# Mixture-of-experts stage of an audio tower: the search for tokens in two halves of eight experts, gathers of one half beside the search of the other

## The reference

```python
def _L0_ffn_ref(x, gate_w, w1, b1, w2, b2, sw1, sb1, sw2, sb2):
    ...
    logits = jnp.einsum('gsd,de->gse', xg, gate_w)
    probs = jax.nn.softmax(logits, axis=-1)
    flat_probs = probs.transpose(2, 0, 1).reshape(En, T)
    scores, tok_idx = jax.lax.top_k(flat_probs, cap)
    xf = x.reshape(T, Dn)
    toks = xf[tok_idx]
    h = jax.nn.gelu(jnp.einsum('ecd,edh->ech', toks, w1) + b1[:, None, :])
    y = jnp.einsum('ech,ehd->ecd', h, w2) + b2[:, None, :]
    y = y * scores[..., None]
    routed = jnp.zeros_like(xf).at[tok_idx.reshape(-1)].add(y.reshape(-1, Dn))
    shared = jax.nn.gelu(xf @ sw1 + sb1) @ sw2 + sb2
    out = (routed + shared).reshape(Bn, Sn, Dn)
```

## Time and profile before

| | |
|---|---|
| time, median of 3 runs | 1312.71 us (1312.13 to 1312.76) |
| the profiled execution | 1312.21 us |
| its span, first to last instruction | 1310.5 us |
| PE busy | 1181.3 us, 90% |
| DVE busy | 893.2 us, 68% |
| ACT busy | 733.1 us, 56% |
| POOL busy | 405.4 us, 31% |
| mean granted PE clock | 0.958 of full speed |
| block three begins | at 1002.7 us of the span |

### The profile page before, as it was taken

The page is one execution under the profiler, slowest core; times in us unless marked ns, Lnnn a source line. Parts: engine busy times, 40 slices in busy tenths (PEclk is TensorE's granted clock), DMA queues, the critical chain, the costliest instruction groups (busy, mean ns, idle before and its releaser), DMA issues. The chain is left out here.

```text
span 1310.5 us, 23146 instructions
## 1 busy us (share of the span) xinstructions
PE 1181.3 (90%) x7812; PEld 992.7 (76%) x7812; DVE 893.2 (68%) x2614; ACT 733.1 (56%) x1847; POOL 405.4 (31%) x379
## 2 busy tenths in 40 slices
PE   6999999999988999999999999999996998766663
PEld 6999999999966777777777777777764767555553
DVE  5656566656659898898998888988864887222120
ACT  2444534444448888888888888888882342222220
POOL 5000001202003442333344324231111001788885
PEclk9999999999999999999999999999997999878876
DMA  5100000000000000000000000000002110445442
GB/s 141 33 13 23 15 16 21 13 24 13 1 25 13 11 16 27 26 26 27 26 20 15 21 27 26 25 14 12 11 21 56 30 33 20 83 91 91 90 90 22
DMA packets 91799, 42.92 MB, mean 33 GB/s; under 512 B 31066, under 2 KB 88007, under 8 KB 91687
## 3 DMA queue, kind: packets, MB, share of 16 engines
q1 hardware_dynamic: 67207, 33.49, 9.4%
q0 software_dynamic: 23808, 6.69, 4.0%
q10 hardware_dynamic: 672, 1.31, 0.3%
HBM read 28.22 MB, written 9.65 MB: 29 GB/s over the span
## 5 line engine op out<-in xcount | busy, mean ns | idle before, releaser
L492 PE MATMUL bank<-h1hl,W2hl 128*128 128x376 f32 x1536 | 277.1, 336 | 2.9 <-DVE h1hl L648 2.9
L492 PEld LDWEIGHTS bank<-h1hl,W2hl 128*128 128x128 f32 x1536 | 263.4, 189 | 7.4 <-issue 4.3
L228 POOL TENSOR_SCALAR cellmax<-grid,csb 125x375 f32<-125x375 f32 x96 | 121.1, 1272 | 392.9 <-DVE csb L221 336.8
L1095 ACT ACTIVATE P<-P,nmax 125x375 f32<-125x375 f32 (+2 forms) x384 | 189.0, 509 | 2.4 <-DVE nmax L1236 2.2
L592 ACT ACTIVATE h<-bank,b2c 128x375 f32<-128x375 f32 x128 | 73.5, 575 | 207.1 <-PE bank L492 207.1
L1236 DVE CUSTOM_DVE_ANT_0 P<-bank,nbias 125x375 f32<-125x375 f32 (+2 forms) x384 | 139.0, 411 | 12.0 <-PE bank L913 12.0
L1105 ACT COPY PT<-bank 128x500 f32<-128x500 f32 (+1 forms) x256 | 128.5, 556 | 8.6 <-PE bank L926 7.9
L913 PE MATMUL bank<-QK 64*125 64x375 f32 (+2 forms) x768 | 116.2, 406 | 13.0 <-DVE nmax L1236 13.0
L926 PE MATMUL bank<-ident,P 125*128 125x125 f32 x768 | 113.5, 275 | 0.2 <-ACT PT L1105 0.2
L1714 ACT ACTIVATE hE<-bank,EB 128x375 f32<-128x375 f32 x64 | 36.7, 573 | 135.0 <-PE bank L1663 132.3
L1121 ACT ACTIVATE tap<-bank,qkd 128x375 f32<-128x375 f32 x128 | 68.5, 570 | 65.3 <-PE bank L962 65.2
(11 more groups left out here) (218 smaller groups left out, 2264.1 us busy)
## 6 DMA issues: line engine op xcount, KB each, us to landing
X<-in_x_dram SPq DMA_DIRECT2D x31, 375.0 KB
EW<-in_L_ffn_w_dram SPq DMA_DIRECT2D x32, 256.0 KB
token_table<-row SPq DMA_DIRECT2D x16, 210.9 KB
tTall<-tT SPq DMA_DIRECT2D x16, 187.5 KB, 2.5
out_dram<-oS SPq DMA_DIRECT2D x15, 187.5 KB
tTall<-in_L_tok_W_dram ACTq DMA_DIRECT2D x1, 1024.0 KB, 8.9
EB<-in_L_ffn_b_dram SPq DMA_DIRECT2D x16, 62.5 KB
tok<-token_table,ids POOLq DMA_INDIRECT x48
```

Source lines behind the costliest of these rows:

```text
L228: nc.gpsimd.tensor_scalar(cellmax[:, k % 2], grid0[:], csb[:, TT_ + k:TT_ + k + 1], None, ALU.max).then_inc(s_cm, 1)
L492: last = nc.tensor.matmul(bank[4 + m % 2][:, :NE], W2hl[:, a, k, m * 128:(m + 1) * 128], h1hl[:, p, b, k], start=(k == 0 and n == 0), stop ...
L1095: nc.scalar.activation(P[:, 2 * r + q, SEG[i]:SEG[i] + w], P[:, 2 * r + q, SEG[i]:SEG[i] + w], ACT.Exp, bias=nmax[:, 2 * r + q, i:i + 1], ...
```

## The change

- Two halves: `GE` = 8 experts each. `probsT` has a partition for each of 8 experts and 16 sequences, 2 x 375 columns, one half of the experts beside the other. Each sequence's probabilities are stored by two DMAs. Search, selection and lists are made for half 0, then for half 1, each over 375 columns (`over`, `tied`, `ties`, `chosen`, `place`); `hotA` and `hotB` are made for 384 columns once per half.
- `STEP_UNITS` puts 1 or 2 shared units between totals in the first search (after `FIRST_UNITS` = 2 ahead of the first total), 2 in the second; 7 stand beside the one-hot matrices of half 0.
- GpSimd issues the 24 gathers of half 0 at once when its lists are ready (`RING` = 8 buffers). The gathers of half 1 go two per expert behind the scatters of experts 2 to 13.
- Lists of half 1: the selection comes ahead of expert 0; `hotA`, `hotB` and `pass_tiles` stand between DVE's steps of experts 0 and 1, and `collect`, `transpose_lists`, `make_indices` on TensorE between experts 1 and 2.
- Experts: no run-time loop. The first layer uses two PSUM banks in turn, the second layer two others: third 0 in one, thirds 1 and 2 in the other. The bias is a matmul with a row of ones on TensorE. DVE multiplies by the score, read in place from `tok`, on the way from PSUM, third by third, and a scatter waits for its own third. No copies of indices or scores.
- Shared sums go from PSUM into `Hall` by DVE and are stored from there; `oS` and ScalarE's copies are gone.
- In block two `shared_y` stands after the projection (h = 3 of the last round) and no longer after the logits (h = 7).

```diff
+                        if (b, h) == (B, 3):
+                            shared_y(0, 0)
+                            shared_y(0, 1)
...
-                        if (b, h) == (B, 7):
-                            shared_y(0, 0)
-                            shared_y(0, 1)
...
-                        sp.dma_start(probsT[m // 2 * E:(m // 2 + 1) * E, m % 2 * N:(m % 2 + 1) * N], pTs[:]
-                                     ).then_inc(s_ps, 16)
+                        for half in range(2):
+                            sp.dma_start(probsT[m * GE:(m + 1) * GE, half], pTs[half * GE:(half + 1) * GE]
+                                         ).then_inc(s_ps, 16)
...
-            STEP_UNITS = [(k + 1) * 45 // STEPS for k in range(STEPS)]
+            FIRST_UNITS = 2
+            STEP_UNITS = ([FIRST_UNITS + 3 * (k + 1) // 2 for k in range(STEPS)],
+                          [33 + 2 * (k + 1) for k in range(STEPS)])
+            LIST_UNITS = ((25, 32, 33), (UNITS,))
+            B_FROM = 2
...
-                for e in range(AHEAD):
-                    gather(e, e)
+                for n in range(NT * GE):
+                    gather(n // NT, n % NT)
...
+                for e in range(E):
+                    scatter(e)
+                    for n in range(2 * (e - B_FROM), 2 * (e - B_FROM + 1)):
+                        if 0 <= n < NT * GE:
+                            gather(GE + n // NT, n % NT)
...
+                def second_layer(e):
+                    u = e % 2
+                    pe.wait_ge(s_ehr, 4 * e + 4)
+                    for t in range(NT):
+                        y = Y_B[min(t, 1)][:PT_, t * C:(t + 1) * C]
+
+                        if t < 2:
+                            wait(pe, s_ys, NT * (e - 1) + 1 if t == 0 else NT * e)
+                        for k in range(DC):
+                            nc.tensor.matmul(y, hE[:, u, k, t * PT_:(t + 1) * PT_], EW2[:, u, k], start=(k == 0),
+                                             stop=False)
+                        last = nc.tensor.matmul(y, ones_r[0:1, 0:PT_], EB2[0:1, u], start=False, stop=True)
+                        if t != 1:
+                            last.then_inc(s_ey, 1)
+
+                def expert(e):
+                    first_layer(e)
+                    if e + 1 < E:
+                        transpose_tokens(e + 1)
+                    second_layer(e)
...
+                transpose_chosen(1)
+                transpose_tokens(0)
+
+                pe.wait_ge(s_yr, NB)
+                expert(0)
+                expert(1)
+                collect(1)
+                transpose_lists(1)
+                make_indices(1)
+                for e in range(2, E):
+                    expert(e)
...
+                select(1, added, NB)
+                split_places(1)
+                take_tokens(0)
+                hot_a(1)
+                take_tokens(1)
+                hot_b(0, SLOT // 2)
+                weigh(0)
+                hot_b(SLOT // 2, SLOT)
+                take_tokens(2)
+                pass_tiles(1)
+                weigh(1)
+                pick(1)
+                for e in range(2, E):
+                    if e + 1 < E:
+                        take_tokens(e + 1)
+                    weigh(e)
```

588 lines of the change are left out of this document (265 added, 323 removed).

## The result

| | before | after |
|---|---|---|
| time, median | 1312.74 us (4 runs: 1312.13 to 1317.06) | 1331.63 us (4 runs: 1325.8 to 1334.56) |
| ratio | | 1.0131, interval 1.0088 to 1.0175 |
| the profiled execution | 1312.21 us | 1325.8 us |
| its span | 1310.5 us | 1324.1 us |
| mean granted TensorE clock | 0.958 | 0.959 |

The change costs 18.9 us by the medians and 17 by the ratio, which is one of means. It went the way that was forecast, but 15 us further, and above the upper end of the range (1326). The profiled execution is the fastest of the four after; the others are slower, and their mean clock is lower (1329.5 at 0.956, 1333.7 at 0.951, 1334.6 at 0.950). So the miss has two parts: 9.4 us inside the profiled execution (1325.8 against 1312.2 is +13.6, forecast +4.2), and 5.8 us from it to the median, where 0.5 was allowed.

A forecast was written before the change was run, and what follows sets the result against it. TensorE was taken to bound the search and GpSimd's scatter and gather rounds the expert stage. 1312.2 - 3.2 (block start) + 7.1 (to first scatter) - 0.2 (rounds) + 0.5 (port) = 1316.4, median 1316.9 us; range 1307.5 to 1326.

The forecast's parts named there:

- Block start: Third block's start, with shared_y moved behind the last projection: 3.2 us earlier.
- rival 3: Second search: DVE's cand and thr held by gathers, 13 us more, 1329; chance 0.07.
- Rounds with two gathers: Expert stage: the scatter's landing shows behind two gathers, 10.55 us a round, 1.0 less than before.
- rival 1: Expert rounds: gathers hide the scatter's dispatch, round 9.98 us, 1309.6 in all, if idle is under 0.4; chance 0.14.
- First late round: Round to scatter group 13, waiting for expert 14's last gather behind group 12: 15.3 us.
- Start to first scatter: From block start through two searches and lists to the first scatter: 7.1 us later than before.
- End just in time for the third group: Rest of hotB, second lists and collect, between experts 0 and 2, finish without delaying the third scatter group.
- The last rounds: Last three scatter rounds, two of them late for tokens of experts 14 and 15: 15.3, 17.6 and 11.3 us.
- the two other thirds of the layer: Second layer in the late groups: these come later than GpSimd would take them, 0.7 us per group.
- the port: DVE's small operations beside gathers in the second search: 0.5 us more.
- twelve rounds win 12.2 and two lose 11: First to sixteenth scatter group: 170.8 us for 170.98, so 0.2 us less.
- Rival 4: First search: TensorE at the low clock for half the steps, 10 us more, 1327; chance 0.05.

The follow-up runs named there:

- r9_warm: Changed kernel with eight matmuls whose result nobody reads in TensorE's waits beside the lists and before expert 0's first layer; 1326.88 us, ratio 1.0084 to the kernel before.
- r8_lists3: Changed kernel with the second half's collect, transposes and indices one expert later, between experts 2 and 3; 1329.05 us, ratio 1.0099 to the kernel before.
- r6_nobias: Changed kernel without its bias matmuls, the second bias left out of the result; 1325.33 us, ratio 1.0075 to the kernel before.
- r1_same: The changed kernel again, unaltered; 1334.12 us, ratio 1.0128 to the kernel before.
- r2_tail: Changed kernel with three gathers behind experts 2 and 3, then two, the last behind expert 12 instead of 13; 1322.21 us, ratio 1.0045 to the kernel before.
- r10_best: Changed kernel with the edits of r2_tail, r8_lists3 and r9_warm, and one more unread matmul behind each collect; 1312.78 us, ratio 0.9987 to the kernel before.
- r12_fills: r9_warm's kernel with one more unread matmul behind each half's collect; 1329.70 us, ratio 1.0104 to the kernel before.
- r3_fill: Changed kernel with unread matmuls in the first search, behind the two first totals and in steps with one shared unit; 1334.47 us, ratio 1.0138 to the kernel before.

## Why the prediction was wrong

The step that failed is the price of TensorE's work behind a wait. The sum put the first lists and expert 0's first layer at the high clock, took what stands ahead of expert 2 to be hidden, and gave the last two thirds of a late expert's layer 0.7 us. The rows show the first at the low clock (3.5 us more up to the first scatter), the second on the path (2.5 us more in the second round), and 3.0 us for the third, with its bias matmuls.

**Right:** the sign, and the structure of the sum. Block start: 3.2 us earlier was forecast; shared_y alone gave 2.4 of the time. The 4.3 of the profile has 1.7 of spread in it, since the projection ended that much earlier than in the profile of before. The second search took 40.0 us for 14 steps with 24 gathers beside it, to the tenth as computed. The counts took 600 to 603 ns beside gathers and 599 to 603 without, the updates of `thr` 152 and 154, the new `cand` 221 and 222 ns (medians): rival 3 falls, DVE was not held. The Trainium skill (SBUF — State Buffer, the section on who interferes with whom) states that a DVE instruction with two SBUF inputs contends with a GpSimd instruction that reads SBUF. For these operations beside indirect gathers the trace shows no such hold; whether a gather is such an instruction, no run here shows. Rounds with two gathers: 10.55 was forecast; the eleven even ones took 10.2 to 11.3, median 10.6; the idle time behind the second gather is 0.5 to 1.6 us, so rival 1 (under 0.4) falls as well. First late round: 15.3 forecast, 15.2 measured.

**Wrong, in the profiled execution, 9.4 us:**

- *Start to first scatter, 10.6 for 7.1.* The chain of the searches was right; the clock was not. The first total came 1.5 us sooner than put down (4.2 for 5.7), then the first search's 14 steps took 42.3 for 40.0, with 1.9 of it in one step of 4.82. First gather at 73.7 us after the start (71.4 forecast), the second search's last total at 114.4 (112.1), first scatter at 135.0 (131.5). In the first lists two groups of shared units, put down at 2.8 and 1.4 us, took 3.5 and 2.5 behind a wait of 1.91; the first layer of expert 0, put down at 2.9, took 4.49. I had costed both stages at the high clock. r9_warm takes back 1.6 of this in its profile, all of it behind the second search, and shows the layer at 3.06.
- *The second round, 13.0 for 10.5.* "End just in time for the third group" was the step: six bias pairs and the second lists stand ahead of expert 2, and the term was never summed. r8_lists3 (10.3) removes it; r6_nobias (10.7) does too, with 1.4 more in the first round.
- *The last rounds, 48.5 for 44.2.* The late tokens cost what was computed, but the two other thirds of the layer were put down at 0.7 us a group, and cost 3.0 (3.27 and 3.29 idle against 0.30). The second third has no signal of its own; it is reported with the last third, so at the low clock and with two bias pairs its scatter waits through two thirds, not one. Without the pairs (r6_nobias) the three scatters of these groups take 4.7 and 5.2 us instead of 7.6.
- *The rest:* 0.5 in the eleven even rounds and 0.3 at the end, 0.5 less for the port, and 1.1 less by the block start. The prediction's line that twelve rounds win 12.2 and two lose 11 does not give its own 0.2: by the rows of before (138.5 and 32.5 us) it forecast 11.9 won in twelve rounds and 11.7 lost in three.

**Wrong, outside it, 5.8 us for 0.5.** I took the median to lie 0.5 above the profiled run, as before. The kernel before spreads over 6.7 us too when 17 executions are seen (1311.7 to 1318.4); three within 0.6 us had hidden that. Both profiled executions are fast ones, but not by as much: that of before lies 3.7 us below the median of the 17, that of after 8.3 below that of r1_same. Whether the changed kernel spreads wider is not shown (7.2 us in the six runs of r1_same), but low-clock stretches that come and go now lie on its path: r1_same, 8.5 us longer in its span, has 2.0 of it ahead of the first scatter and 2.9 in the second round. Rival 4 named the low clock, but for the steps of the first search and at a chance of 0.05; there it cost 2.3 us, and the lists, expert 0 and expert 2 took the rest.

**What the change is.** The gain it aims at, rounds shorter by one us each, came in eleven of the twelve (10.6 for 11.5 in the median). r2_tail and r8_lists3 repair two faults of order, r9_warm covers the waits, and with all three the kernel is 1.7 us faster than before (0.9987); but the kernel before with only shared_y moved is 2.4 us faster (0.9982), and the two intervals overlap. Eight us more to the first scatter, with two searches in a row, stay in r10_best (132.3 against 124.4) and eat what the rounds give.

## What to carry to other kernels

When gathers are moved from a queue's busy stage to an earlier one, count when the last of them is issued, not only how many stand behind each step: three of 48 (expert 14's last, expert 15's last two) issued one group too late cost 11 us here. When transfers that ran beside an engine's slow stretch are moved away (gathers beside TensorE's restart behind the lists), price that stretch at the low clock. Giving each third of the split result its own signal looks worth doing by the 3.3 us pauses; it was not tried. Take the spread from many runs before a forecast's last term is the distance from a profile to a median.

## What the runs showed of the hardware

- A bias matmul with one row takes more than its share of rows would say: 0.41 us per pair of instructions at the high clock and 0.71 at the low one, where eight instructions with 128 rows take 1.07 and 1.85 (from start to start). I had put it at 0.23.
- A scatter group that must wait for the one before cost 10.2 us at least, with two gathers behind it or with none: three issues of 2.3, and 3.7 to 4.0 from the end of the last of them to the next scatter.
- Twenty-four indirect gathers back to back beside a search did not lengthen VectorE's operations there: medians differ by at most 3 ns, the longest `thr` update is 195 ns for a median of 152.
- Eight matmuls that nobody reads, 5.5 us of TensorE's time at full clock, made the kernel 5.8 us faster; with two more of them (r12_fills) it was 3.2. Thirteen in the first search alone gained nothing (r3_fill): the low clock came back in the stage behind it.
